# Layer 0's update made token by token from tile 7 on, and turned back through DRAM and VectorE

## What is computed

```python
# layer 0: one adapter per sequence, rank 16
Bx = einsum('bni,bri->bnr', x, B0[adapter_ids])
x  = x + einsum('bnr,bor->bno', Bx, A0[adapter_ids])
# layer 1: a dense layer and a gated mixture of 8 LoRA experts, rank 16
base   = x @ W.T
logits = x @ Wr.T + 5.0 * one_hot(language_ids)
gates  = softmax over the two largest logits, 0 elsewhere
h      = einsum('btd,erd->bter', x, A)
x      = x + base + 2 * einsum('bter,bte,eor->bto', h, gates, B)
```

## Time and profile before

| | us |
|---|---|
| Median of 3 runs | 535.11 (534.6 to 536.44) |
| Profiled execution | 534.09 |
| Its span, from first to last instruction | 532.3 |
| Mean granted TensorE clock | 0.994 of full |
| PE busy | 521.4 (98%) |
| DVE busy | 326.7 (61%) |
| ACT busy | 210.6 (40%) |
| POOL busy | 173.1 (33%) |

### The profile page before, as it was taken

One profiled execution on the slowest core, in us unless ns is written; L12 is line 12 of the kernel. 1 busy time (PEld: TensorE's weight loads), 2 busy tenths in 40 slices (PEclk: granted clock), 3 DMA queues, 4 the chain that ended last, 5 costly groups with the idle time before them and its releaser, 6 DMA issues.

```text
span 532.3 us, 9378 instructions
## 1 busy us (share of the span) xinstructions
PE 521.4 (98%) x3500; PEld 478.2 (90%) x3500; DVE 326.7 (61%) x829; ACT 210.6 (40%) x493; POOL 173.1 (33%) x162
## 2 busy tenths in 40 slices
PE   5999999999999999999999999999999999999997
PEld 5888899998999999899998989999898999989897
DVE  4888676655567665556765555685555667555321
ACT  3646433425344242525424353443435334343211
POOL 6462222434331343422234342223433223341100
PEclk9899999999999999999999999999999999999999
DMA  8933523444332444433244433324443333421101
GB/s 330 321 102 98 154 89 89 129 129 129 89 116 77 107 128 129 115 99 107 68 129 129 129 109 97 104 79 129 128 123 99 101 102 94 129 89 41 41 40 41
DMA packets 30865, 60.42 MB, mean 114 GB/s; under 512 B 4316, under 2 KB 20060, under 8 KB 30820
## 3 DMA queue, kind: packets, MB, share of 16 engines
q1 hardware_dynamic: 24144, 38.81, 24.0%
q0 software_dynamic: 6656, 20.98, 13.5%
q10 hardware_dynamic: 20, 0.03, 0.0%
HBM read 43.02 MB, written 16.78 MB: 112 GB/s over the span
## 4 chain that ended last, share of the span: by engine, by line
PE 88%; DVE 7%; ACT 2%; issue 1%; POOL 1%; DMA 0%; ACTq 0%; DVEq 0%
PE o_bank L469 70%; PE o_bank L482 8%; PE x_bank L388 4%; PE b_bank L370 3%; DVE a_raw L746 1%; DVE x_bank L728 1%; PE b_bank L358 1%; DVE w_lo L703 1%; DVE x_lo L703 1%; ACT bx_pair L617 1%; DMA ids<-in_itok_B_dram 0%; PE o_bank L458 0%; PE o_bank L358 0%; DVE top_no L806 0%; POOL a_in L274 0%
## 5 line engine op out<-in xcount | busy, mean ns | idle before, releaser
L469 PE MATMUL o_bank<-w_hi,x_hi 128*128 128x512 f32 (+1 forms) x744 | 257.0, 345 | 0.0
L469 PE MATMUL o_bank<-w_lo,x_hi 128*128 128x512 f32 (+1 forms) x744 | 251.4, 338 | 0.0
L469 PE MATMUL o_bank<-w_hi,x_lo 128*128 128x512 f32 (+1 forms) x744 | 251.3, 338 | 0.0
L299 POOL TENSOR_TENSOR a_t<-a_raw,a_t 64x1024 fp32r<-64x1024 f32 x30 | 72.1, 2402 | 282.7 <-ACT a_t L590 282.7
L469 PEld LDWEIGHTS o_bank<-w_hi,x_hi 128*128 128x128 f32 x744 | 141.0, 189 | 12.2 <-issue 3.0
L469 PEld LDWEIGHTS o_bank<-w_hi,x_lo 128*128 128x128 f32 x744 | 139.8, 188 | 10.2
L469 PEld LDWEIGHTS o_bank<-w_lo,x_hi 128*128 128x128 f32 x744 | 140.2, 188 | 8.9
L599 ACT COPY xt<-x_bank 128x512 f32<-128x512 f32 x64 | 37.6, 587 | 122.6 <-DVE x_bank L728 119.6
L728 DVE STREAM_TRANSPOSE x_bank<-x_in 128x512 f32<-128x512 f32 x60 | 68.4, 1186 | 0.0
L274 POOL DMA_INDIRECT a_in<-in_L_cond_A_dram,a_run x64 | 60.9, 951 | 19.2 <-issue 19.1
L746 DVE STREAM_TRANSPOSE a_raw<-a_in 128x1024 f32<-128x1024 f32 x32 | 63.5, 1985 | 0.0
(11 more groups left out here) (102 smaller groups left out, 486.0 us busy)
## 6 DMA issues: line engine op xcount, KB each, us to landing
out_dram<-out_sb SPq DMA_DIRECT2D x31, 512.0 KB, 2.9
x_in<-in_x_dram SPq DMA_DIRECT2D x120, 128.0 KB, 3.5
w_in<-in_L_cond_W_dram SPq DMA_DIRECT2D x6, 512.0 KB, 8.7
x_in<-in_x_dram SPq DMA_DIRECT2D x2, 512.0 KB, 3.3
out_sb<-in_L_cond_W_dram SPq DMA_DIRECT2D x2, 512.0 KB, 15.1
a_in<-in_L_cond_A_dram,a_run POOLq DMA_INDIRECT x64, 3.4
w_in<-in_L_cond_A_dram SPq DMA_DIRECT2D x1, 512.0 KB, 4.4
b_in<-in_L_cond_B_dram,b_run POOLq DMA_INDIRECT x32, 2.9
```

The lines of the kernel that those rows point to most:

```text
L299: nc.gpsimd.tensor_tensor(lower, a_raw[Q:P, :], lower.bitcast(F32), ALU.subtract).then_inc(a_lo_ready, 1)
L469: mm = pe.matmul(O[part][:, 0:hi - lo], xs[:, n % 2, c, :], w[:, c, lo:hi], start=(k == 0), stop=(k == K3 - 1), skip_group_check=True)
```

## The change

From tile K = 7 on the update of layer 0 is made the other way round. `make_delta` takes `bx_t` as the weights and moves `a_t`: two matmuls of 512 columns give the update with tokens on partitions, in the banks `X[1]`. ACT copies it to `d_sb`, SP stores it to a DRAM buffer and loads it back into `dq` in the layout of x, POOL adds x (`add_delta`), DVE turns the sum into `x1_t` in SBUF, and ACT and DVE make hi and lo from there. x itself is turned by DVE into `xt` in SBUF, so the xt copies on ACT go. The A transposition has another column order from tile 7 on. `a_raw` and `a_t` have two buffers, x_in four. The update of tile n+2 is made in tile n; the B products and sums are made in odd tiles for n+2 and n+3. In DVE's order the B sums, the choice and the weights stand ahead of the turn of x1. The gated turn comes after all of part 1. Before tile 7 the old way is kept, with some operations in another place. POOL's gathers stand behind the addition.

```diff
+    XS = 4
+    K = 7
+    d_rows = nc.dram_tensor("d_rows", [2, P, D], F32, kind="Internal").ap()
-        x_in = sb("x_in", [P, 2, G, F])
+        x_in = sb("x_in", [P, XS, G, F])
-        a_raw = sb("a_raw", [P, D])
+        a_raw = sb("a_raw", [P, 2, D])
-        a_t = sb("a_t", [P, D], F32R)
+        a_t = sb("a_t", [P, 2, D], F32R)
+        d_sb = w_in[:, 0, :]
+        dq = w_in[:, 1, :].rearrange("p (g f) -> p g f", g=G)
+        x1_t = w_in[:, 2, :].rearrange("p (k m) -> p k m", k=C)
+        DB = X[1]
...
-            return tuple(m for m in (n + 1, n + 2) if n % 2 == 0 and m < T)
+            if n < K - 2:
+                return (n + 1, n + 2) if n % 2 == 0 else ()
+            return tuple(m for m in (n + 2, n + 3) if n % 2 == 1 and m < T)
...
+            def reload_x(m):
+                if m < XS + 2:
+                    sp.wait_ge(x_psum, HB * (m - XS + 1))
+                elif m - XS < K:
+                    sp.wait_ge(xT_ready, HB * (m - XS - 1))
+                else:
+                    sp.wait_ge(x1q_ready, m - XS - K + 1)
+                load_x(sp, m)
+
+            def turn_delta(m):
+                j = m - K
+                sp.wait_ge(d_copied, HB * (j + 1))
+                sp.dma_start(d_rows[j % 2], d_sb).then_inc(d_stored, 16)
+                sp.wait_ge(d_stored, 16 * (j + 1))
+                if j > 0:
+                    sp.wait_ge(x1t_ready, HB * j)
+                rows = d_rows[j % 2].rearrange("(g i) d -> i g d", i=SQ)
+                for c in range(NQ):
+                    sp.dma_start(dq[c * SQ:(c + 1) * SQ, :, :],
+                                 rows[:, :, c * F:(c + 1) * F]).then_inc(dq_loaded, 16)
+            for n in range(T):
+                for m in x_tiles(n):
+                    reload_x(m)
+                if K <= n + 2 < T:
+                    turn_delta(n + 2)
+                if n < T - 1:
...
...
+            def add_delta(m):
+                j = m - K
+                pool.wait_ge(dq_loaded, 16 * NQ * (j + 1))
+                pool.wait_ge(x_loaded[m % XS], x_count(m))
+                nc.gpsimd.tensor_tensor(dq[:, :, :], dq[:, :, :], x_in[:, m % XS, :, :], ALU.add).then_inc(x1q_ready, 1)
+            for m in range(3, T):
+                a_lo_part(m, min(m + (1 if m <= K else 2), T - 1), min(m + 1, T - 1))
+                pool.wait_ge(a_lo_ready, m + 1)
+                if m - 1 >= K:
+                    add_delta(m - 1)
+                    pool.wait_ge(x1q_ready, m - K)
+                if m == K:
+                    reload_b(m + 2)
+                if (m + 2 if m < K else m + 3) < T:
+                    reload_b(m + 2 if m < K else m + 3)
+                if m + 2 < T:
+                    reload_a(m + 2)
+            add_delta(T - 1)
...
+            def make_delta(m):
+                j = m - K
+                pe.wait_ge(bx_step, bx_count(m + 1))
+                pe.wait_ge(a_lo_ready, m + 1)
+                for h in range(HB):
+                    if j > 0:
+                        pe.wait_ge(d_copied, HB * (j - 1) + h + 1)
+                    pe.matmul(DB[h][:, :], bx_t[:, m % 2, :], a_t[:, m % 2, h * BANK:(h + 1) * BANK],
+                              start=True, stop=True).then_inc(d_psum, 1)
...
-                if n + 1 < T:
+                if n + 1 < K:
                     add_l0(n + 1)
-                make_part(n, 1, 0, 18)
+                if K <= n + 2 < T:
+                    make_delta(n + 2)
+                make_part(n, 1, 0, K3)
                 turn_gated(n)
-                make_part(n, 1, 18, K3)
...
+            def d_copy_part(m):
+                j = m - K
+                if j > 0:
+                    act.wait_ge(d_stored, 16 * j)
+                for h in range(HB):
+                    act.wait_ge(d_psum, HB * j + h + 1)
+                    nc.scalar.copy(d_sb[:, h * BANK:(h + 1) * BANK], DB[h][:, :]).then_inc(d_copied, 1)
...
+            def turn_x_half(m, h):
+                dve.wait_ge(x_loaded[m % XS], x_count(m))
+                dve.wait_ge(bx_psum, m - 1)
+                src = x_in[:, m % XS, :, :].rearrange("p g (j k) -> p k g j", k=C)
+                nc.vector.transpose(xt[:, m % 2, chunks(h), :].rearrange("p k (g i) -> p k g i", i=SQ),
+                                    src[:, chunks(h), :, :]).then_inc(t1_ready, 1)
+
+            def turn_x1_half(m, h):
+                dve.wait_ge(x1q_ready, m - K + 1)
+                dve.wait_ge(x1_lo_ready, HB * m)
+                src = dq[:, :, :].rearrange("p g (j k) -> p k g j", k=C)
+                nc.vector.transpose(x1_t[:, chunks(h), :].rearrange("p k (g i) -> p k g i", i=SQ),
+                                    src[:, chunks(h), :, :]).then_inc(x1t_ready, 1)
```

More of the change, by code:

```diff
@@ L139, in two_adapter_layers @@
         ids_row, ids_psum = map(sem, ("ids_row", "ids_psum"))
-        x_loaded = [sem(f"x_loaded{k}") for k in range(2)]
+        x_loaded = [sem(f"x_loaded{k}") for k in range(XS)]
         a_loaded = [sem(f"a_loaded{k}") for k in range(2)]
@@ L231, in load_x @@
             for c in range(NQ):
[L232 to L233 removed]
+                eng.dma_start(x_in[c * SQ:(c + 1) * SQ, m % XS, :, :],
+                              rows[:, :, c * F:(c + 1) * F]).then_inc(x_loaded[m % XS], 16)
         block = ctx.enter_context(nc.Block())
@@ L345, in _ @@
             load_b(2)
[L346 to L352, removed]
+            pool.wait_ge(a_lo_ready, 2)
+            reload_b(3)
+            reload_a(3)
+            pool.wait_ge(a_lo_ready, 3)
+            reload_b(4)
+            reload_a(4)
+            for m in range(3, T):
[11 more added lines that the diff above has]
+            add_delta(T - 1)
         @block.tensor
@@ L688, in _ @@
                     a_hi_part(2)
-                    xt_part(3)
+                if n == K - 4:
+                    a_hi_part(n + 2)
+                if n % 2 == 0 and n >= K - 1:
+                    for m in a_tiles(n):
+                        a_hi_part(m)
                 exp_part(n)
-                if n + 1 < T:
+                if n + 1 < K:
                     x1_hi_part(n + 1)
[L693 to L698, removed]
+                for m in old_turned(n):
+                    xt_part(m)
+                if K <= n + 2 < T:
+                    d_copy_part(n + 2)
+                if K <= n + 1 < T:
+                    x1_hi_part(n + 1)
+                out_part(n, 0)
+                out_part(n, 1)
+                if n == K - 4:
+                    a_hi_part(n + 3)
+                elif n < K - 1 or n % 2 == 1:
+                    for m in a_tiles(n):
+                        a_hi_part(m)
+                out_part(n, 2)
         @block.vector
@@ L932, in _ @@
             for n in range(1, T):
-                for m in bx_tiles(n):
+                turn_again = K <= n + 1 < T
+                if n >= K - 1 and n % 2 == 0:
+                    for m in turned(n)[0:1]:
+                        for h in range(HB):
+                            turn_x_half(m, h)
+                    for m in a_tiles(n):
+                        aT_part(m)
+                if n == K - 4:
+                    aT_part(n + 2)
+                for k, m in enumerate(bx_tiles(n)):
                     bx_half_part(m)
+                    if n == K - 3:
+                        turn_x_half(n + 3, k)
                     bx_rest(m)
@@ L937, in _ @@
                     a_lo_part(2)
-                    xT_part(3)
                 choose_experts(n)
                 weigh_experts(n)
+                if turn_again:
+                    turn_x1_half(n + 1, 0)
+                    if n % 2 == 1:
+                        gated_t_part(n)
+                    turn_x1_half(n + 1, 1)
+                    if n % 2 == 0:
+                        gated_t_part(n)
+                if n == 1:
+                    xT_part(3)
                 if n + 1 < T:
                     x1_lo_part(n + 1)
[L943 to L951, removed]
+                if not turn_again:
+                    gated_t_part(n)
+                for m in old_turned(n)[1:] if n == 1 else old_turned(n):
+                    xT_part(m)
+                for m in turned(n)[1:]:
+                    for h in range(HB):
+                        turn_x_half(m, h)
+                for m in b_tiles(n):
+                    bT_part(m)
+                if n == K - 4:
+                    aT_part(n + 3)
+                elif n < K - 1 or n % 2 == 1:
+                    for m in a_tiles(n):
+                        aT_part(m)
 _INS = ["x", "itok_B_4_50", "itok_B_0_7", "L0_cond_A", "L0_cond_B", "L1_cond_W", "L1_cond_Wr", "L1_cond_A", "L1_cond_B"]
```

100 lines of the change are left out of this document (70 added, 30 removed).

## The result

The changed kernel takes **541.76 us** (539.62 to 543.33, 4 runs) against 535.13 us before (534.6 to 536.44), a ratio of 1.0114 with a 95% interval of 1.0096 to 1.0133. It is slower, by 6.6 us. The forecast was 532.8 us and faster; what came is the second rival (542.4 us), at the place and in the manner that it named, though not all of the loss came from there.

A forecast was written before the change was run, and what follows sets the result against it. PE was taken as the bound, busy 521.4 us, 98% of the span. From 534.09 us, 9.5 gained by PE and 7.2 lost to meetings gave 531.8, or 532.8 us on the median's footing; range 524.5 to 542.

The forecast's parts named there:

- the second rival: Additions cost more than PE gains, at bx_all or bx_own of odd tiles: 1.4 us a pair, 542.4 us; chance 0.28.
- PE's gain: Layer-0 update from tile 7 on takes 0.46 us instead of 0.84: 9.5 us over 25 tiles, pair 30.56 us.
- Where the addition falls: POOL's addition was to run 11.8 to 14.2 us after an even tile's part 0, meeting bx_all.
- the walk: Step-by-step timing from E, end of an even tile's part 0, past M, end of the next B products, E+10.15.
- The price per pair: In odd tiles bx_all waits 1.6 us for POOL's addition; PE stops 0.6 us per pair, bounds 0.3 to 1.1.
- the slack of 1.0: Odd tile: gates ready 8.7 us after the B products end, PE wants them at 9.7, leaving 1.0 us.
- the 7.2 us of the sum: PE's total stop from additions meeting the B sums: 0.6 us in each of 12 pairs, 7.2 us.
- 0, at worst 0.2: Even tile: top_no waits for the earlier addition just its slack of 1.0 us, costing PE 0, at worst 0.2.
- B's deadline: Even tile: DVE's work through B's transposition takes 8.7 us after part 0, PE asks for B at 9.7.
- Tiles 1 to 6 get a new order only. I cost that at nothing: First tiles: gates' extra 0.9 us helps 1.1 us of late gates; x's earlier transposition takes as much back, net nothing.
- DVE not the bound, the gathers and reloads covered: DVE at 23.7 us a pair is nearly full, not the bound; late gathers and reloads cost nothing.
- my ends: A half transposition on DVE into SBUF was put between 1.01 and 1.19 us, making 27.4 to 28.1 a pair.

The follow-up runs named there:

- the first run: The changed kernel with the B sums (half, all, own) written to free columns of PSUM bank O[2], so none reads two SBUF tiles: 523.42 us, ratio 0.9792.

## Why the prediction was wrong

**PE's gain**: right, and somewhat low. The new update takes 0.46 to 0.47 us against 0.84, as reckoned. The pair bound by PE is 30.39 us, not 30.56: part 1, the turn and the first half of part 2 take 3.52 + 0.11 + 1.80 us, where an even tile took 2.69 + 0.18 + 2.69. Where nothing is lost to the port, in the first run, 11.1 us are gained between medians, not 9.5 (9.2 between the two traces, each of one execution).

**Where the addition falls**: right within 1.3 us in the tile shown, later over the run. The walk's stations in the kernel after, tile 16: part 0 in the chain, the earlier addition on POOL, the store and the first load on SP:

```profile
287.46 5.50 PE o_bank L582 x24
```

```profile
292.34 2.41 POOL L377 TENSOR_TENSOR w_in<-w_in,x_in 128x1024 f32<-128x1024 f32 x1
```

```profile
296.58 0.43 SPq L315 DMA_DIRECT2D d_rows<-w_in  x1
301.56 1.74 SPq L321 DMA_DIRECT2D w_in<-d_rows  x4
```

E is 292.96. The earlier addition ends at E+1.8, as walked. The store goes at E+3.6 (4.0 in the walk), but the loads can follow only 5.0 us later, not 2.9, with the x loads just ahead of the store; the addition (306.07) starts at E+13.1, not 11.8, and M is E+10.6. It therefore met now bx_all, now one of the three behind it. Over the 12 even tiles the addition starts 12.6 to 15.5 us after the update's first matmul, which follows E at once (13.3 in this one), 13.8 on average, 2 us behind the walk. The mean wait in odd tiles is 1.6 us, the very value I took. That is luck: the addition came later and met other instructions than the one I priced.

**The price per pair**: this is the step that failed, "It waits 1.6, less the slack of 1.0: PE stops 0.6 us per pair". Measured, the pair loses 31.93 - 30.61 = 1.3 us, 1.0 in the odd tile and 0.3 in the even one; the 7.2 us of the sum were 14.6. Four things were missing. First, a mean was put in where the loss isn't linear: waits of 0.5 to 0.8 us cost 0.1 (tiles 9, 19 and 25), those of 1.6 to 2.7 cost themselves less about 0.7. This is the smaller part: priced one by one with the slack of 1.0, the waits of tiles 7 to 27 give 0.8 instead of 0.6. Second, PE takes the turn in 0.33 us when it had to wait for it and 0.11 when not (chains above), 0.2 us for each stop. Third, the even tile's top_no was given a slack of 1.0 and "0, at worst 0.2"; its wait of 0.8 to 1.0 (1.3 in tile 8) reaches the first LoRA term instead, which stands at 1.22 us in place of 0.95 in this row of the chain after:

```profile
331.16 1.22 PE o_bank L595 x6
```

There I had watched only B's deadline, though the gated copy now stands behind both halves of x1. Fourth, the B products wait a little too (1.16 us for 1.01).

**"Tiles 1 to 6 get a new order only. I cost that at nothing"**: wrong by 3.1 us, the second step that failed. The A transposition of tile 6 ends late, ACT's cast stands ahead of the swap there, the swap waits another 1.03 us for something unknown, and a_lo meets bx_hi (2.37 us). The first run has the same transposition and cast, without the other two, and loses nothing in the change-over (47.5 us). An a_lo at the same port was in my rows; I looked for it only in the new tiles.

**DVE not the bound, the gathers and reloads covered**: right; with the sums in PSUM DVE is busy 392.9 us of 523.1 and PE alone bounds. A half transposition into SBUF took 1.15 to 1.18 us on average, 1.03 to 1.1 with the overlap, between my ends.

**Rival 2** had the place and price ("bx_all or bx_own of an odd tile", from 0.79 a pair), and lost in my chances because I left the store's landing at 2.9 us, where it took 4.4; the loads' 3.0 was right (2.9 as the median). Its sentence that POOL waits once bx_all has begun to read didn't help: in tile 17 the addition started as bx_all ended and took bx_own. That its 542.4 us came so close to 541.76 is in part luck: it lacks the 3.1 us of the change-over, and its gain of PE is too small.

The sum with measured terms: -11.1 gained, +14.6 in eleven pairs (11 x 1.33) and +3.2 in the change-over (50.7 less 47.5) come to +6.7; measured +6.6. The first term is between medians, the others are between the traces of the changed kernel and of the first run. Between traces alone it is -9.2 + 14.6 + 3.2 - 0.3 (the start) = 8.3, the difference of the spans. This says that nothing large was lost elsewhere; it doesn't test the terms one by one.

## What to carry to other kernels

An engine's slack is not one number: before work goes to GpSimd, list which VectorE instructions on the path read two SBUF tiles, or cast from SBUF to SBUF, and ask for each whether it can meet it; a tiny one waits as long as a big one. Here the cure was cheaper than a better schedule: one operand in PSUM took the cost of the meetings away (541.8 to 523.4 us), while moving the operation in time left a part of it (535.8, the store first) or chose a worse victim (548.3, the addition after the sums). And waits that vary are priced one by one against the slack, not by their mean, and each stop of PE has a price of its own.

## What the runs showed that I had not expected

- An instruction of 128x1 elements waited 2.17 us for POOL (weight, above).
- A 512 KB store took 4.4 us to land with four x loads right ahead of it, and 2.7 without them (medians).
- The sums in PSUM cost the kernel before 0.43% and gave the changed one 3.2%. Why the old kernel loses 0.3 us in every second even tile wasn't followed.
- Starting the new way two tiles earlier cost 5 us more by the median of four runs that lie 5.1 us apart, where 0.9 less was expected.
- Late in the run a_lo of tile 31 follows an addition at once and stops weight in tile 28 (16.45 us for that tile with the sums in PSUM, 14.61 for its like). A version in which the choice of experts is free of the port as well wasn't tried.
- ACT stood 1.0 to 1.4 us ahead of a swap in the first tiles of some traces, released by nothing that the profile names. It is on the chain of the changed kernel; why it comes and goes is open.
